# First attention of a two-layer kernel: another order of its row tiles, and no first passes of one head alone

## The reference, cut to what matters

```python
latent_kv = x @ w_kv_down
k, v = split(latent_kv @ w_kv_up)          # 16 heads of 64 each
q = x @ w_q
att = einsum('bqhd,bkhd->bhqk', q, k) * 64 ** -0.5
att = softmax(where(causal, att, -inf))
y = einsum('bhqk,bkhd->bqhd', att, v).reshape(B, T, 1024) @ w_out
# the layer: x + attention(layernorm(x)) + fp4_ffn(layernorm(x))
```

## Time and profile before

| what | us |
|---|---|
| median of 3 runs | 2287.49 (2284.92 to 2288.25) |
| the profiled execution, its own time | 2287.97 |
| its span from first to last instruction | 2286.2 |
| PE busy | 2154.7 (94%) |
| DVE busy | 1672.4 (73%) |
| ACT busy | 1322.8 (58%) |
| one turn with a preparation (500.29 to 542.41) | 42.12 |

### The profile page before, as it was taken

One profiled execution on the slowest core, in us unless ns is written; L12 is line 12 of the kernel. 1 busy time (PEld: TensorE's weight loads), 2 busy tenths in 40 slices (PEclk: granted clock), 3 DMA queues, 4 the chain that ended last, 5 costly groups with the idle time before them and its releaser, 6 DMA issues. The chain is left out here.

```text
span 2286.2 us, 45447 instructions
## 1 busy us (share of the span) xinstructions
PE 2154.7 (94%) x19387; PEld 1343.7 (59%) x19387; DVE 1672.4 (73%) x2210; ACT 1322.8 (58%) x2126; POOL 47.6 (2%) x61
## 2 busy tenths in 40 slices
PE   4999999999999999999999989999999999999998
PEld 2666666676776766767667666544444444444444
DVE  6777777777767777677777775777777777777771
ACT  3655556555565555655556553466666666666666
POOL 5000000000000000000000000100000000000000
PEclk7999999999999999999999999999999999999999
DMA  5000000000000000000000019100001111001000
GB/s 123 1 1 1 1 1 1 1 1 1 1 1 1 1 1 1 1 1 1 1 1 1 1 35 231 48 20 20 20 20 30 27 29 32 20 20 20 11 2 11
DMA packets 41211, 42.60 MB, mean 19 GB/s; under 512 B 21361, under 2 KB 33617, under 8 KB 40882
## 3 DMA queue, kind: packets, MB, share of 16 engines
q1 hardware_dynamic: 39858, 39.05, 7.5%
q10 hardware_dynamic: 1152, 0.64, 0.1%
HBM read 27.71 MB, written 11.70 MB: 17 GB/s over the span
## 5 line engine op out<-in xcount | busy, mean ns | idle before, releaser
L1733 DVE TENSOR_REDUCE nm_half<-slot 128x2 f32<-128x1024 f32 x512 | 606.5, 1222 | 162.8 <-PE slot L1511 118.0
L1714 ACT ACTIVATE pT<-slot 128x1024 f32<-128x1024 f32 x512 | 505.9, 1026 | 270.6 <-PE slot L1620 215.9
L948 ACT ACTIVATE prob<-slot,negmax 128x1024 f32<-128x1024 f32 (+6 forms) x448 | 316.8, 718 | 255.1 <-DVE negmax L1045 181.8
L752 PE MATMUL slot<-k_hl,q_hl 64*128 64x512 f32 (+3 forms) x2560 | 356.1, 359 | 57.7 <-ACT prob L948 54.9
L752 PEld LDWEIGHTS slot<-k_hl,q_hl 64*128 64x128 f32 x2560 | 259.4, 186 | 99.2 <-ACT prob L948 74.3
L790 PEld LDWEIGHTS slot<-ident,prob 128*128 128x128 f32 x2304 | 253.9, 141 | 88.7 <-issue 61.4
L790 PE MATMUL slot<-ident,prob 128*128 128x128 f32 x2304 | 288.6, 275 | 0.9 <-DVE probT L612 0.9
L612 DVE COPY probT<-slot 128x768 f32<-128x768 f32 (+1 forms) x192 | 166.8, 869 | 151.3 <-PE slot L790 148.6
L802 PE MATMUL yspace<-probT,v_sb 128*64 128x512 f32 (+3 forms) x1536 | 276.2, 494 | 0.0
L1586 PE MATMUL yspace<-pT,v 128*32 128x512 f32 x2048 | 266.9, 603 | 1.6 <-ACT y_raw L1701 0.8
L1614 PE MATMUL slot<-qs,ks 49*128 49x512 f32 x1024 | 240.2, 471 | 15.1 <-DVE nm_half L1733 7.5
(11 more groups left out here) (244 smaller groups left out, 2330.3 us busy)
## 6 DMA issues: line engine op xcount, KB each, us to landing
qs<-q_hi SPq DMA_DIRECT2D x64, 64.0 KB
qs<-q_lo SPq DMA_DIRECT2D x64, 64.0 KB
ks<-k_hi SPq DMA_DIRECT2D x64, 64.0 KB
ks<-k_lo SPq DMA_DIRECT2D x64, 64.0 KB
x_tok<-in_L_attn_x_dram SPq DMA_DIRECT2D x4, 512.0 KB, 6.6
q_hi<-qk_out SPq DMA_DIRECT2D x4, 512.0 KB, 4.4
q_lo<-qk_out SPq DMA_DIRECT2D x4, 512.0 KB, 5.3
k_hi<-qk_out SPq DMA_DIRECT2D x4, 512.0 KB, 6.1
```

Source lines behind the costliest of these rows:

```text
L752: nc.tensor.matmul(own_ps[a][:, o:o + m], q_hl[hq][own, i * P:(i + 1) * P], k_hl[hk][own, o:o + m], start=(k == 0), stop=(k == 3 and o + m ...
L948: last = nc.scalar.activation(prob[a][:, p_at(i, 0, w)], ps[:, o:o + w], ACT.Exp, bias=negmax[:, i, a:a + 1], accum_out=sums[:, i, a:a + 1])
L1714: nc.scalar.activation(pT[hp][m % PT_DEEP][:, :, :], slot[at["x", n] % RING][:, :].rearrange("p (j t) -> p j t", t=BANK), ACT.Exp)\
L1733: nc.vector.tensor_reduce(nm_half[:, h, :, p * TPB + i], slot[pos % RING][:, :].rearrange("p (a t) -> p a t", t=BANK), AX.X, ALU.max, nega ...
```

## The change

The order of the row tiles becomes 4, 7, 6, 3, 5 and then 0, 1, 2; the ring, its slots and the two tasks in the output space keep their places. So tasks 0, 1 are row tile 4, tasks 2, 3 row tile 7 (its second head in the output space), tasks 4, 5 row tile 6, task 6 row tile 3, and tasks 7, 8 row tile 5 (its second head in the output space). The first passes of a single head go; all four passes are of both heads, behind the claims of both slots. PE's calls follow the new numbers. DVE and ACT read `s_list` and keep their code.

```diff
-                s_list = [(7, 0), (7, 1), (6, 0), (6, 1), (3, None), (5, 0), (5, 1), (4, 0), (4, 1), (0, None), (1, None), (2, None)]
+                s_list = [(4, 0), (4, 1), (7, 0), (7, 1), (6, 0), (6, 1), (3, None), (5, 0), (5, 1), (0, None), (1, None), (2, None)]
...
-                LONE = {5: 1, 7: 1}
...
-                            passes = range(4)
...
-                            elif n in LONE:
-
-                                for a in range(2):
-                                    own_ps[a] = score_claim(n + a)[:, 0:w]
-                                    for k in range(LONE[n]):
-                                        one_pass(k, (a,))
-                                passes = range(LONE[n], 4)
...
-                            for k in passes:
+                            for k in range(4):
                                 one_pass(k, range(2))
...
-                        scores(5)
+                        scores(6)
                         scores(7)
```

## The result

| | before | after |
|---|---|---|
| median, us (6 runs each) | 2287.71 | 2278.91 (2275.11 to 2280.74) |
| ratio to before | 1 | 0.9961, interval 0.9948 to 0.9974 |
| the profiled execution | 2287.97 | 2280.74 |
| its span | 2286.2 | 2278.9 |

The kernel is faster by 8.8 us where 17 were forecast: the way was right, the size half. The median lies in the range that was given (2262 to 2283).

A forecast was written before the change was run, and what follows sets the result against it. The first part of a turn was taken as bound by a PE, DVE, ACT, PE loop, the second by PE. 0.60 us in 32 turns, 19.2, less 2.1 for preparation, gave 17.1 us: 2270.5, range 2262 to 2283.

The forecast's parts named there:

- Steps 1 to 6: First part of a turn, tiles 4, 7, 6, 3, 5 through PE, DVE and ACT: last releases at 13.24 us.
- ACT's lead: ACT at the gates: takes them at 13.14 us of the turn instead of 13.44, so 0.30 ahead.
- The lone passes: One pass of a single head removed in tile 4 (0.06 us) and one in tile 5, lying in a PE wait.
- Step 7: PE at the end of the first part: gates at 10.30 us, `turned(0)` at 13.37 against 14.01; 0.64 gained a turn.
- What must follow: From the gates to score task 9: ACT allows 0.59 us, 0.60 taken a turn, 19.2 us in 32 turns.
- cover of 0.29: ACT's copy 0 ended 0.29 us before PE needed it for score task 9; counted as wholly usable.
- ACT's tail binds: Rival: ACT's last exponentials limit the turn, only its lead of 0.30 us counts; 2280 us, chance 0.14.
- Preparation: DVE operations before tile 4's maxima: 0.05 us late in 12 turns, 0.25 in 6; 2.1 us back.
- the prediction's bounds: Unmeasured widths of tiles 4, 5 and 6: gains of 0.34 to 0.82 us a turn, 2264 to 2279 us.
- The sign that was named for ACT's tail: A bracket of more than 0.2 us before score task 9 or `turned(0)` would speak for that rival.
- Tile 7: Rival: its start, forecast at 1.45 us, comes late because slot 2 frees late; 2302 us with 1.2 late, chance 0.07.
- Nothing measurable: Rival: each of three crossings PE, DVE, ACT costs 0.2 us more than its rows; about 2287 us, chance 0.07.

The follow-up runs named there:

- e2: The kernel before, with the lone first passes of tiles 4 and 5 both taken out: 2292.11 us, ratio 1.0020.
- e6: The kernel before, with the lone first pass of tile 5 out and that of tile 4 kept: 2293.20 us, ratio 1.0028.
- e5: The changed kernel, with the copies of gu and of the values moved to DVE, ACT keeping the exponential of the gates: 2274.52 us, ratio 0.9943.
- e4: The changed kernel, with DVE's end-of-turn preparation and moments moved behind the maxima of task 8 of the next turn: 2274.35 us, ratio 0.9943.
- e7: The changed kernel, with tile 5 computed head by head, head 0 in the output space while PE waits for slot 0: 2272.71 us, ratio 0.9937.
- e9: The changed kernel run again, unaltered: 2279.07 us, ratio 0.9964 to the kernel before.
- e1: The changed kernel, with copy 0 given to DVE and copy 1 to ACT: 2276.09 us, ratio 0.9953.

## Why the prediction was right in its way and wrong in its size

- **Steps 1 to 6, the loop of the first part.** Right, each within 0.14. The two small errors are tile 6's start, 0.07 or 0.08 late, and its width from PE to DVE, 2.02 instead of 1.96; tile 5's width, the one without a row, came at 1.81 for 1.84. They make ACT's lead at the gates 0.20 and not 0.30, PE's 0.56 and not 0.64.
- **The lone passes.** Their price in a usual turn was right (0.06 reckoned for tile 4, 0.08 for both by e2). The 0.27 that the prediction gives for a whole pass of 640 columns is smaller than its rows: four such passes take 1.36, or 0.34 each. What was missed is what the one in the wait did for the clock in the old order (e2, e6). In the new order without them the loop shows no such fall beyond the first turn, so it cost this change nothing there.
- **Step 7 and "What must follow": the step that failed.** The prediction held that ACT's lead of 0.30 and its cover of 0.29 ahead of score task 9 allow 0.59 a turn. It followed ACT's tail to copy 0 only. The slots of gates and values are freed by the same tail, and `turned(1)` and `turned(2)` need them sooner: counted at their first weight loads (14.77 and 15.64 of the turn in the kernel before, ACT's ends 14.54 and 15.46) and less the 0.05 of the hand-over, the covers are 0.18 for the gates and 0.13 for the values, not 0.29. PE catches up some 0.05 behind a late load. So ACT allows, as an estimate from these rows, its lead and 0.18 more: 0.48 a turn with the forecast lead of 0.30, and 0.38 with the measured one of 0.20, which is what a clean turn won. The rival "ACT's tail binds" (2280) is what happened, at another place than the text named: 0.22 a turn, 7 us in all (of which 0.08 is `turned(0)` later than forecast, and 0.18 the waits inside the transposes, less the 0.04 already allowed for ACT; e5 gives 0.16 of these back, 2.73 against 2.89).
- **Preparation.** Right for the turns it named (e4: 3.3 us with two turns more); the two behind moments were missed, 1.1 us.
- **The first turn.** Not in the prediction: 0.8 us longer instead of 0.6 shorter in the profiled execution, through the clock.
- 7.0, 1.1 and 1.4 make 9.5 of the 9.9 us between 17.1 forecast and 7.2 in the profiled pair. The 7.0 count the first turn once more (0.2), the named preparation cost 0.2 less than reckoned, and the part behind the loop, 0.8 longer, is the rest.
- **Where luck helped.** The median lies at the bad end of the prediction's bounds (2279), but these were for the widths of tiles 4, 5 and 6, which came out near the values taken. The loss has another cause that no bound was made for. The sign that was named for ACT's tail, a bracket of more than 0.2 ahead of score task 9 or `turned(0)`, did not show, although ACT's tail was the limit.
- **Rivals.** Tile 7 came at 1.50 with no wait, right behind tile 4: that rival is out. "Nothing measurable" by slower crossings is out too: the three crossings cost some 0.1 in all more than their rows.

## What to carry to other kernels

Where a gain moves one engine ahead of another, list every slot that the slower engine frees behind the gained stretch, and take the smallest margin, counted at PE's weight loads, not that of the task that looks last; margins of a few hundredths that are met leave no bracket, only a longer merged row. Work that only fills a wait can be worth nothing in time by the rows (e7) and still hold the granted clock (e2, e6): before taking it out, ask what PE does in its place. And work of another engine that ends in the cover of a large first task loses that cover when a small task is put first; move it where the engine is idle (e4).

## What the runs showed of the hardware

- The granted clock fell to half (1.2 GHz) within a loop in which PE is over 90% busy. It did so behind PE's waits of 0.71 and 0.92 in a turn of e2 (turn 11), in 10 of 32 turns of e2 and 7 of e6, at about 1 us a fall, with the same waits in turns that show no fall. The changed kernel has waits of 0.65 and 1.12 in each turn and no fall in the loop outside its first turn. What tells these apart was not found.
- One kernel has the clock at half for 6.8 us of the first turn in one execution and 3.4 in another (the changed kernel and e9); the turn takes 42.69 and 41.24, and 39.98 at full clock (e1). That is a good part of the spread between executions, and more than some of the edits bring.
- Four passes of one head alone over 768 columns take as long as four passes of both heads (1.70 and 1.71 to the next task, e7), so the two row halves of PE do run at the same time. The Trainium skill, "TensorEngine Tiling (Array Packing)", Tiling Modes, states that tiles operate independently; this case's trace agrees. The prediction's rows showed only 0.06 lost for a lone pass of tile 4, and there the second head's matmul starts 0.11 behind the first (509.65 against 509.54), which would explain it.
